# Attention maxima of a group spread over two groups of the schedule, and gamma and beta on VectorE in the first stage

## The reference

```python
# layer 0: gated linear attention over chunks of 64, then residual + LayerNorm, then the MoE's own LayerNorm
x = layernorm(x + gla(x))
normed = (x - mean) * rsqrt(var + 1e-5) * ln_gamma + ln_beta      # input of router, shared FFN and experts
...
# layer 1: differential attention, 16 heads, two score maps per head, causal
a1 = softmax(q1 @ k1.T * scale + mask); a2 = softmax(q2 @ k2.T * scale + mask)
o  = rmsnorm_per_head(a1 @ v - lam * (a2 @ v)) * (1 - lambda_init)
x  = layernorm(x + o @ Wo.T + bo)
# then a top-2 MoE, residual, LayerNorm
```

## Time and profile before

| what | us |
|---|---|
| median of 3 runs (lowest, highest) | 2336.41 (2335.39, 2339.7) |
| the profiled execution's own time | 2334.71 |
| its span, first to last instruction | 2333.0 |
| TensorE busy | 2158.9 (93%) |
| VectorE busy | 1576.2 (68%) |
| ScalarE busy | 1233.2 (53%) |
| GpSimd busy | 675.3 (29%) |

### The profile page before, as it was taken

The page is one execution under the profiler, slowest core; times in us unless marked ns, Lnnn a source line. Parts: engine busy times, 40 slices in busy tenths (PEclk is TensorE's granted clock), DMA queues, the critical chain, the costliest instruction groups (busy, mean ns, idle before and its releaser), DMA issues.

```text
span 2333.0 us, 50379 instructions
## 1 busy us (share of the span) xinstructions
PE 2158.9 (93%) x17816; PEld 1352.9 (58%) x17816; DVE 1576.2 (68%) x2696; ACT 1233.2 (53%) x2365; POOL 675.3 (29%) x765
## 2 busy tenths in 40 slices
PE   7999999889999999995776899999999999999998
PEld 5788777456666666664654344444444444447886
DVE  4666666643333333335989999989989998925878
ACT  5656565213333323332331599988888888863110
POOL 1111111102333333333557133343243243222000
PEclk9999999989999999997987799999999999998999
DMA  4323324652222222223333011101002001200000
GB/s 138 127 101 120 107 99 182 216 195 43 55 36 37 38 37 36 36 35 133 125 139 138 20 59 35 38 30 59 34 30 61 32 30 47 66 20 1 28 19 28
DMA packets 90042, 163.96 MB, mean 70 GB/s; under 512 B 16224, under 2 KB 64352, under 8 KB 88144
## 3 DMA queue, kind: packets, MB, share of 16 engines
q1 hardware_dynamic: 76176, 141.98, 17.7%
q0 software_dynamic: 13632, 18.77, 5.0%
HBM read 99.70 MB, written 60.49 MB: 69 GB/s over the span
## 4 chain that ended last, share of the span: by engine, by line
PE 56%; DVE 16%; ACT 3%; issue 3%; DMA 1%; SPq 0%; POOL 0%; DVEq 0%; ACTq 0%
PE PS L2272 9%; DVE NM L2156 9%; PE PS L1448 8%; PE PS L58 6%; PE PS L60 6%; PE PS L59 6%; PE PS L2352 6%; PE PS L2296 4%; PE PS L1433 2%; DVE TT L1641 2%; DVE X L2544 2%; PE PS L2226 1%; PE PS L2291 1%; PE PS L2317 1%; DVE PP L1624 1%
## 5 line engine op out<-in xcount | busy, mean ns | idle before, releaser
L2156 DVE TENSOR_REDUCE NM<-PS 128x2 f32<-128x1024 f32 (+3 forms) x608 | 673.1, 1163 | 57.7 <-PE PS L2296 54.2
L2059 ACT ACTIVATE E<-PS 128x512 f32<-128x512 f32 (+2 forms) x1280 | 625.3, 556 | 92.6 <-PE PS L2352 77.6
L2272 PE MATMUL PS<-E,VP 128*32 128x256 f32 (+1 forms) x5120 | 364.1, 370 | 6.0 <-ACT OT L2093 2.3
L1993 POOL TENSOR_SCALAR_AFFINE_SELECT E<-E 128x512 f32<-128x512 f32 x256 | 163.3, 638 | 376.0 <-ACT E L2059 374.9
L1245 DVE SCALAR_TENSOR_TENSOR XIL<-PS,XSC,XIH 128x128 f16<-128x128 f32 x142 | 43.3, 346 | 335.6 <-ACT XIH L1041 335.6
L1076 ACT ACTIVATE HB<-PS 128x768 f32<-128x768 f32 x71 | 57.5, 810 | 301.0 <-PE PS L1433 301.0
L2272 PEld LDWEIGHTS PS<-E,VP 128*32 128x32 f32 x5120 | 111.1, 108 | 171.9 <-issue 85.9
L2352 PE MATMUL PS<-QK 50*128 50x512 f16 (+3 forms) x1152 | 196.7, 332 | 6.1 <-ACT E L2059 4.0
L1448 PE MATMUL PS<-WALL,HB 128*128 x852 | 195.7, 379 | 1.0 <-ACT HB L1076 1.0
L2296 PE MATMUL PS<-QK 48*128 48x512 f16 (+3 forms) x1152 | 185.2, 342 | 6.3 <-DVE NM L2156 6.0
L985 POOL DMA_INDIRECT XB<-x_normed,IDX x71 | 70.9, 999 | 365.6 <-DVE GAT L1261 315.8
(11 more groups left out here) (354 smaller groups left out, 3993.2 us busy)
## 6 DMA issues: line engine op xcount, KB each, us to landing
parts<-PP SPq DMA_DIRECT2D x32, 512.0 KB, 3.0
WIN<-in_we SPq DMA_DIRECT2D x16, 768.0 KB, 5.3
QK<-parts SPq DMA_DIRECT2D x96, 128.0 KB
WALL<-pairs_of_weights SPq DMA_DIRECT2D x7, 1536.0 KB
pairs_of_weights<-WPH SPq DMA_DIRECT2D x16, 384.0 KB, 2.4
pairs_of_weights<-WPL SPq DMA_DIRECT2D x16, 384.0 KB, 3.3
WALL<-in_we SPq DMA_DIRECT2D x8, 768.0 KB
QK<-parts SPq DMA_DIRECT2D x96, 64.0 KB
```

The source lines that it names most:

```text
L1993: e.affine_select(out=E[:, m % NE, :, 0:128], in_=E[:, m % NE, :, 0:128], pattern=[[0, 4], [1, 128]], compare_op=ALU.is_ge, fill=0.0, base ...
L2059: e.activation(dst, src, ACT.Exp, scale=unit).then_inc(S.ex, 1)
L2156: e.tensor_reduce(dst, src, AX, ALU.max).then_inc(S.mx, 1)
L2272: a = e.matmul(PS[32 * jj:32 * jj + 32, 7, 512 - n + c0:512 - n + c1], VP[b % 2][:, kt, 17 * hd:17 * hd + 32], E[:, m % NE, jj, c0:c1], st ...
```

## The change

It has three parts.

1. First stage: VectorE writes the rows in two `scalar_tensor_tensor` per batch, `(x - mean) * GAM` and then `* rstd + BET`; GpSimd's two instructions and the half of VectorE in tile 8 are gone; `n2` is gone. ScalarE instead of VectorE copies the transposed rows to NTT in tiles 1 to 7, ahead of its squares. `XTL` moves behind the 16 state updates.
2. Attention: another `STEPS` table, other orders of the 19 units and of the woven-in tables; `EARLIER = 13` delays the maxima by 13 units, so that 6 units of group w + 2 and 13 of group w + 1 stand in group w; the row work (r, R, L) of group w + 1 moves from steps 0 to 3 to steps 15 to 17 of group w. The bias is added in 16 instructions of 128x512, one in each of the groups 1 to 16 at step 14.
3. Waits that an earlier one of the same engine already covers are dropped (`qk_ld`, `row_ld`, `vp_ld`, `pe_av`).

```diff
@@ gla, pool @@
-            if t > 0:
-                e.wait_ge(S.n2, u + 1)
...
-                n = own.pool.on(e.tensor_tensor(nav[:, 0:nb, u, :], nav[:, 0:nb, u, :], GAM[:].unsqueeze(1).to_broadcast([128, nb, 256]), ALU.mult))
-                e.wait_ge(own.pool.sem, n)
-                e.tensor_tensor(nav[:, 0:nb, u, :], nav[:, 0:nb, u, :], BET[:].unsqueeze(1).to_broadcast([128, nb, 256]), ALU.add).then_inc(S.nr, 1)
@@ gla, act: behind high(2 * t + 1), ahead of the squares @@
+                if t > 0:
+                    for k in HALF:
+                        e.wait_ge(S.pe_nt, 2 * u + k + 1)
+                        if u > 0:
+                            e.wait_ge(S.pe_x1, u + 2)
+                        e.activation(NTT[:, k], rows(PS[:, out_banks(t)[2][k], :]), ACT.Copy).then_inc(S.ntt, 1)
@@ gla, dve @@
-                layernorm_apply(e, K, xu, [nav[:, b, u, :] for b in QUAD])[-1].then_inc(S.n2, 1)
-            if t < 7:
-                e.wait_ge(S.xhi, t + 2)
-                e.tensor_tensor(XTL[:], XTS[(t + 1) % 2][:], XTH[:].bitcast(F32), ALU.subtract).then_inc(S.xlo, 1)
+                for b in QUAD:
+                    n = own.dve.on(e.scalar_tensor_tensor(out=nav[:, b, u, :], in0=xu[b], scalar=K.MV[:, b, 0:1], in1=GAM[:], op0=ALU.subtract, op1=ALU.mult))
+                for b in QUAD:
+                    e.wait_ge(own.dve.sem, n - 3 + b)
+                    a = e.scalar_tensor_tensor(out=nav[:, b, u, :], in0=nav[:, b, u, :], scalar=K.RS[:, b:b + 1], in1=BET[:], op0=ALU.mult, op1=ALU.add)
+                a.then_inc(S.nr, 1)
@@ gla, dve: behind the 16 state updates @@
-                if t > 0:
-                    turn_out()
+                if t < 7:
+                    e.wait_ge(S.xhi, t + 2)
+                    e.tensor_tensor(XTL[:], XTS[(t + 1) % 2][:], XTH[:].bitcast(F32), ALU.subtract).then_inc(S.xlo, 1)
@@ attention, tables @@
-        "rRsmm", "svm", "svvmOx", "smLv", "sxhH", "s", "s", "smv", "smv", "smxv", "sxmvovm", "sv", "sdmm",
+        "smm", "svv", "sxmvmO", "smv", "shmdH", "s", "s", "sxvm", "svv", "smv", "somvm", "sxmxv", "smvA",
...
+    EARLIER = 13
+    biased = 14
-    squared = {(0, 16 + i): i for i in range(8)}
+    squared = {(0, 13 + i): i for i in range(8)}
...
+    def unit_at(w, k):
+        n = NU * (w + 2) + k - EARLIER
+        return divmod(n, NU) if 0 <= n < 32 * NU else None
-        if c == "m" and w + 2 < 32:
-            turn(("max", w + 2, k), S.mx, NU * (w + 2) + k + 1)
-        if c == "r" and 1 <= w < 31:
+        if c == "m" and unit_at(w, k):
+            v, u = unit_at(w, k)
+            turn(("max", v, u), S.mx, NU * v + u + 1)
+        if c == "r" and -1 <= w < 31:
             turn(("rows", w + 1), S.mhi, w + 2)
@@ attention, pool @@
-        for b in QUAD:
-            e.tensor_tensor(X[:, 8 * b:8 * b + 8, :], X[:, 8 * b:8 * b + 8, :], BO[:].unsqueeze(1).to_broadcast([128, 8, 256]), ALU.add).then_inc(S.bo, 1)
+        def add_bias(q):
+            x = X[:, 2 * q:2 * q + 2, :]
+            e.tensor_tensor(x, x, BO[:].unsqueeze(1).to_broadcast([128, 2, 256]), ALU.add).then_inc(S.bo, 1)
+            if c == "end" and 1 <= w < 17 and s == biased:
+                add_bias(w - 1)
@@ attention, sp: the rows' stores now stand behind the loads of Q and K in a group @@
-            if w >= 1 and w + 1 < 32:
-                put_rows(w + 1)
             if w >= 0 and w + 3 < 32:
                 fetch(e, w + 3)
-            if w < 0:
-                put_rows(w + 2)
+            if -1 <= w < 31:
+                put_rows(w + 1)
```

More of the change, by code:

```diff
@@ L1784, in attention @@
     some += [[last(i, y) for y in HALF] for i in (1, 5)] + [[last(i, y) for y in HALF for i in (0, 4)]]
-    units = [some[k] for k in (15, 18, 12, 10, 1, 7, 6, 16, 0, 9, 8, 17, 2, 13, 3, 4, 5, 14, 11)]
+    units = [some[k] for k in (16, 4, 0, 3, 1, 9, 12, 8, 15, 18, 13, 2, 5, 11, 14, 17, 10, 6, 7)]
     halves = [(0, 0), (0, 1), (1, 0), (1, 1), (2, 0), (3, 0)] + [(4 + k // 2, k % 2) for k in range(12)] + [(10, 0), (11, 0)]
+    EARLIER = 13
     OVER = 3
@@ L2050, in exponentials @@
                 e.wait_ge(S.pe_sc, i + 1)
-                if m >= NE:
+                if m >= NE and i == exps_to(m):
                     e.wait_ge(S.pe_av, m - NE + 1)
@@ L2197, in dve @@
         for w, s, c, k in steps():
-            if c == "m" and w + 2 < 32:
-                maximum(w + 2, k)
-                if k == NU - 1:
-                    combine(w + 2)
-                    if w == -2:
-                        differences()
-                    if w == -1:
-                        factors()
+            if c == "m" and unit_at(w, k):
+                v, u = unit_at(w, k)
+                maximum(v, u)
+                if u == NU - 1:
+                    combine(v)
+            if c == "m" and k == NU - 1:
+                if w == -1:
+                    differences()
+                if w == 0:
+                    factors()
             if c == "d" and w >= 1:
@@ L2267, in products @@
                     e.wait_ge(S.ex, exps_to(m + 1))
-                e.wait_ge(vp_ld[b % 2], 16 * (b // 2 + 1))
+                if g == 0 and m % 12 == 0:
+                    e.wait_ge(vp_ld[b % 2], 16 * (b // 2 + 1))
             c0, c1 = (256 * half, min(n, 256 * half + 256))
@@ L2347, in scores @@
                         e.wait_ge(*free)
-                    e.wait_ge(row_ld[w % 4], 64 * (w // 4 + 1))
+                    if s == 0 and y == 0 and x == 0:
+                        e.wait_ge(row_ld[w % 4], 64 * (w // 4 + 1))
                     if i == 0:
@@ L2361, in pe @@
         for w, s, c, k in steps():
[L2362 to L2365 removed]
+            if c == "m" and unit_at(w, k):
+                maximum(*unit_at(w, k))
             if c == "s" and w >= 0:
```

59 lines of the change are left out of this document (22 added, 37 removed).

## The result

| | before | after |
|---|---|---|
| median of 4 runs (lowest) | 2337.12 (2335.39) | 2303.97 (2302.83) |
| profiled execution | 2334.71 | 2302.83 |
| its span | 2333.0 | 2301.1 |

The ratio of the times is 0.9858 (95% interval 0.9840 to 0.9875). One of the four runs after took 2337.7, at a mean granted clock of 0.92 where the other three have 0.965 to 0.967, and is left out of the ratio. The kernel is faster, by 33 us; I had forecast 2291, that is 45. The range of 2274 to 2310 holds the time, but the forecast's own range of 2283 to 2299 does not. The span fell by 31.9. It is laid out by four marks in both traces: the first reduction of attention, the first scores, the first scores of group 30, and the last product with V.

The account below looks back on a forecast made before the run. TensorE was taken to bound the kernel nearly everywhere, VectorE one stretch of 49 us. Terms -14 - 20 + 1 - 6 - 6 = -45 gave 2289.7, with 1.7 for the median 2291; range 2274 to 2310, the forecast's own 2283 to 2299.

Parts of the forecast that it names:

- First stage: Tile ends before attention: rows made on VectorE are ready before TensorE's products end; -14 us, bounds -14.5 and -10.
- GpSimd's wait goes entirely: First stage: TensorE's transposes no longer wait for GpSimd's rows, a wait of 14.5 us in 7 places.
- rival E: First stage: the wait only changes its name, state updates or XTL late, 1.5 of 2.2 given back; 2302, chance 7%.
- Start of attention: First reduction to first scores: scores need only 19 reductions and 6 more; -20 us, bounds -15 to -21.
- the lambda sums are hidden in group 0: Start of attention: the lambda sums, 1.3 us, move into group 0, where VectorE is busy 21.9 of 26.3, at no cost.
- The 13 units moved: Groups 30 and 31: group 30 takes the 13 units, up to 5 us, and loses 3 of waits; +1, bounds -3 and +5.
- Tenth group and its like: Groups w = 9, 17, 25: squares move three steps earlier and the waits go; 3 x -2.0 = -6, bounds -9 and 0.
- The other groups: The other 28 attention groups: VectorE is fed more evenly; -0.2 each, -6 in all, bounds -0.8 and +0.5 each.
- A: Attention groups: row work lands too late for the next group's scores, making the kernel slower; 2347 at 1.8 late, chance 3%.
- B: Attention groups: the new order fits worse, bunched reductions costing 0.5 per group; 2311, chance 12%.
- C: Attention: bias pieces on GpSimd hold up the combine in 16 groups by up to 1.1; 2309, chance 6%.
- D: Attention groups: the new order fits well, gaining 0.8 per group; 2274, chance 17%.

Follow-up runs that it names:

- Experiments 1 and 2: The kernel before with only the first stage's change: 2315.27; the kernel before with only GpSimd's multiplication by gamma left out in the first eight tiles: 2310.28.
- first_only: The kernel before with the change of the first stage alone, attention untouched: 2315.27, ratio 0.9929.
- Experiment 7: The changed kernel with VectorE's lambda sums behind the eleventh unit of group 0 instead of ahead of that group: 2300.54, ratio 0.9856.
- Experiment 5: The changed kernel with its four sums of squares at steps 17 to 20 instead of 18, 20, 22 and 0 of the next group: 2298.40, ratio 0.9844.
- experiment 6: The changed kernel with its 16 bias pieces two at a time in groups 1 to 8 instead of one each in 1 to 16: 2298.75, ratio 0.9849.
- experiment 8: The changed kernel with earlier sums of squares, earlier bias pieces, later lambda sums, and the first normalised pairs at step 17 instead of 9: 2288.26, ratio 0.9807.
- experiment 11: The changed kernel with VectorE's reductions over half the columns of each single-part unit, leaving half the maxima's input out: 2278.95, ratio 0.9758.

## Why the prediction was right in part, step by step

**First stage, predicted -14, measured -22.6.** Mechanism right, term mis-sized. The step that failed is "GpSimd's wait goes entirely" at the price of the wait, 14.5 in seven places. The low clock behind five of the seven waits was in the trace of before, and in the earlier trace rows itself: eight transposes at 1.97 where they take 1.16 at the full clock. I took their 2.0 as their length, and used it again for what comes behind them. Experiments 1 and 2 show the true size: 3.6 in a tile where the clock fell, 20.2 in all at the start of tile 8's transposes (415.57 and 395.36). The other 2.4 arise between there and attention, in stages whose instructions the change does not touch; they come with it in `first_only` too, and I did not trace them to a line. The other steps held, but for one place: rows ready ahead of the products' end, no new wait for the state updates, and 0.40 per new instruction between the two rows that I bounded it by. XTL is late ahead of the second tile, by 1.22, and nowhere else. That is rival E in one tile of seven.

**Start of attention, predicted -20, measured -20.1.** Right in each link: combine 0.17, 1.8 to the first store, first scores 27.2 behind the first reduction. One clause was wrong: that the lambda sums are hidden in group 0 because VectorE is busy for only 21.9 of 26.3 there. They stand at that group's very start, where VectorE is the late one, and the low clock lasted longer (to 14 us behind the first scores, 11 before): group 0 went from 26.34 to 28.44. Experiment 7 gave the 2.0 back in three kernels of four, so the lambda sums are the likely cause and not the shown one.

**The 13 units moved, predicted +1, measured -1.0** for groups 30 and 31 together, within the bounds. Group 30 fell from 37.4 to 32.3 and group 31 rose by 4.1. TensorE's idle time in group 30 went from 3.0 to 0.6, as I had said of its waits.

**Tenth group and its like, predicted -6, measured +5.8.** This is the step that failed in kind. "The squares behind that sum move three steps (3 us) earlier and the waits should go": the squares did move, and were ready seven us ahead, but nothing waited for the squares. The last sum is an instruction of VectorE at a fixed place, and `meant` was the one table of this block that the change left alone. What stands ahead of it on VectorE decides, and that is two reductions, which in the new order come later. Experiment 5 moved the sums and took 2.3 of the 2.4 away in w = 9 and 17, so the cause of the growth is shown. The size was wrong besides. Of the earlier trace rows the 0.73 for the combine ends at 1516.58, ahead of the window of the tenth group: it belonged to w = 8 and its like, and it went as forecast (23.90 to 23.32 each). The window itself has 26.20 - 24.77 = 1.43 of idle time, less than the 2.0 that I took off. And in no kernel with the whole reductions did w = 9 fall under 26.2: with the sums out of the way, TensorE waits for the reductions.

**The other groups, predicted -6, measured +6.2** (+12.0 less 5.8). It has four parts: group 0 +2.1; w = 12 and 14 +2.5, of which 0.87 each is the bias piece that holds VectorE up (experiment 6); w = 1 and the other groups from 11 on that grew +3.8; w = 8, 16, 24 and 10, 18, 26 together -2.2; groups 2 to 7 and 15, 23 about nothing. In w = 12, 14, 20, 22 and 28, 0.4 each is the place of the normalisation: with it at another step they take 25.51, less than before (experiment 8). Why w = 1 and w = 11, 13 and their like grew by 0.7 and 0.3 was not tested and stays open. My step was "feeds VectorE a little more evenly, -0.2 each". In an early group there was next to nothing to gain: TensorE is busy for 23.2 of 23.4 in the earlier trace rows, and even with a third of VectorE's work gone it takes 23.25 (experiment 11). My sum left 17.6 - 6 - 3 = 8.6 us of idle time for these 28 groups, 0.3 each, so -0.2 each asked for most of it, and the bound of -0.8 each for more than there was.

**The rivals.** A did not happen; no first score waited for its row. B (the order fits worse, 2311, 12%) was nearest in effect, but not evenly: the growth is in group 0, in w = 1 and in groups with an output projection. C had the right cause, a bias piece that holds VectorE up, and the wrong victim: not the combine in 16 groups but the normalisation in two, 1.7 in all in place of 17. D did not happen, and E in one tile only. That the time lies within the range is in part luck: without the 8.6 that the first stage gave beyond its term it would have been near 2312.6, outside.

## What to carry to other kernels

Price a wait of TensorE by the granted clock behind it and not by its length: 2.2 us of waiting cost 3.6 here where the clock fell, and a transpose or matmul row that is longer than its twin elsewhere is the sign. When a producer is moved earlier, look for the next instruction in line on the engine that consumes it; if that stands at a fixed place, nothing moves until its own table entry does. And before granting a gain "per group" from better order, list the waits group by group: groups without a wait gave nothing here.
